# Interleaving half layers of eight experts with attention work, and moving the gate decision of a batch into the next batch's block

## What is computed

```
h = conv(x, cos(phases) * w_real - sin(phases) * w_imag)      # (8, 735, 64)
n = layernorm(h)
h = h + softmax((n Wq^T)(n Wk^T)^T / 8) n                     # attention, values are n itself
n = layernorm(h)
logits = n gate_w + gate_b                                    # (8, 735, 16)
weights, index = softmax(top_k(logits, 2))
moe = sum over the two: weight * (relu(n w1[e] + b1[e]) w2[e] + b2[e])
h = h + layernorm(n + moe) * gamma + beta
```

## Time and profile before

| what | us |
|---|---|
| median of 3 runs | 396.76 |
| lowest and highest run | 396.74, 397.37 |
| the profiled execution, whole | 397.81 |
| its span, first to last instruction | 396.0 |
| PE busy | 373.5 (94%) |
| DVE busy | 247.5 (62%) |
| ACT busy | 159.0 (40%) |
| POOL busy | 141.8 (36%) |

### The profile page before, as it was taken

The page is one execution under the profiler, slowest core; times in us unless marked ns, Lnnn a source line. Parts: engine busy times, 40 slices in busy tenths (PEclk is TensorE's granted clock), DMA queues, the critical chain, the costliest instruction groups (busy, mean ns, idle before and its releaser), DMA issues.

```text
span 396.0 us, 6294 instructions
## 1 busy us (share of the span) xinstructions
PE 373.5 (94%) x2222; PEld 244.7 (62%) x2222; DVE 247.5 (62%) x592; ACT 159.0 (40%) x494; POOL 141.8 (36%) x167
## 2 busy tenths in 40 slices
PE   8879999889999999999999999999989999999992
PEld 6336475575658666676667755576657667657660
DVE  3377568874686646763776536765676446967662
ACT  3364253363337533354346543374344453020022
POOL 5110040310661185324761165513860296015062
PEclk9998999999999999999999999999999999999997
DMA  5800000392003940079000980059102969539301
GB/s 156 196 33 0 2 1 2 136 406 112 1 2 85 407 183 2 1 246 397 33 1 11 334 330 0 2 160 407 69 1 65 392 231 357 208 102 407 126 2 40
DMA packets 23135, 55.92 MB, mean 141 GB/s; under 512 B 3776, under 2 KB 5312, under 8 KB 22976
## 3 DMA queue, kind: packets, MB, share of 16 engines
q1 hardware_dynamic: 23104, 55.53, 38.6%
HBM read 53.57 MB, written 1.95 MB: 140 GB/s over the span
## 4 chain that ended last, share of the span: by engine, by line
PE 78%; DVE 9%; ACT 5%; SPq 3%; issue 2%; DMA 2%; POOL 1%; POOLq 0%; ACTq 0%; DVEq 0%
PE mix L1070 22%; PE wide L1070 18%; PE up L1070 17%; PE small L1070 15%; DVE row_max L846 3%; PE wide L1096 2%; ACT probs L629 2%; DMA bet<-beta 2%; PE wide L1193 1%; PE small L1089 1%; PE wide L1145 1%; ACT relu L621 1%; DVE probs L913 1%; ACT cen_sq L584 1%; POOL hidden L363 1%
## 5 line engine op out<-in xcount | busy, mean ns | idle before, releaser
L913 DVE SCALAR_TENSOR_TENSOR hidden<-up,b_neg,gates_all 128x368 f32<-128x368 f32 x128 | 70.8, 594 | 22.2 <-PE up L1070 22.1
L1070 PE MATMUL up<-x,w_hi 128*128 128x368 f32 x198 | 74.5, 376 | 1.7 <-ACT relu L621 1.5
L1070 PE MATMUL mix<-hidden,w2s 128*64 128x368 f32 x400 | 67.4, 475 | 0.7 <-POOL hidden L363 0.6
L488 POOL TENSOR_TENSOR rstd<-var_eps,power 128x6 f32<-128x6 f32 x24 | 31.9, 1329 | 94.1 <-ACT cen_sq L584 94.1
L1070 PE MATMUL up<-x,w_lo 128*128 128x368 f32 x198 | 65.3, 330 | 0.0
L363 POOL TENSOR_TENSOR hidden<-relu,gates_all 128x368 f32<-128x368 f32 x52 | 48.9, 976 | 21.4 <-ACT relu L621 21.4
L1070 PEld LDWEIGHTS up<-x,w_hi 128*128 128x128 f32 x198 | 37.1, 188 | 18.9 <-ACT relu L621 6.2
L1070 PEld LDWEIGHTS mix<-hidden,w2s 128*64 128x64 f32 x400 | 27.5, 136 | 33.0 <-issue 28.3
L629 ACT ACTIVATE probs<-wide 128x736 f32<-128x736 f32 (+2 forms) x48 | 36.5, 780 | 25.3 <-PE wide L1070 25.3
L846 DVE TENSOR_REDUCE row_max<-wide 128x1 f32<-128x736 f32 (+1 forms) x48 | 42.7, 916 | 5.9 <-PE wide L1070 5.6
L584 ACT ACTIVATE cen_sq<-cen 128x65 f32<-128x65 f32 x144 | 34.8, 246 | 8.5 <-DVE cen L860 3.4
(11 more groups left out here) (186 smaller groups left out, 547.5 us busy)
## 6 DMA issues: line engine op xcount, KB each, us to landing
gates_all<-gates_far SPq DMA_DIRECT2D x128, 368.0 KB, 7.7
xt<-x_t SPq DMA_DIRECT2D x8, 375.0 KB, 8.4
out<-outs SPq DMA_DIRECT2D x8, 192.0 KB, 1.9
w_raw<-w SPq DMA_DIRECT2D x2, 512.0 KB, 6.2
w2s<-w SPq DMA_DIRECT2D x1, 512.0 KB, 7.2
gates_far<-gates_t SPq DMA_DIRECT2D x8, 46.0 KB, 1.7
gates_all<-w_real SPq DMA_DIRECT2D x2, 128.0 KB, 2.8
gates_all<-w_imag SPq DMA_DIRECT2D x2, 128.0 KB, 3.3
```

Of the source, the lines that this page charges most:

```text
L488: pool.tensor_tensor(rstd[k][:], var_eps[k][:], power[:], ALU.pow).then_inc(s_rstd[k], 1)
L913: dve.scalar_tensor_tensor(hidden_of(n, e)[:, s, :], up_of(n, e)[s], b1_neg[:, e:e + 1], gates_all[:, e, s * HALF:(s + 1) * HALF], ALU.max ...
L1070: return pe.matmul(dst, lhsT, rhs, start=start, stop=stop, skip_group_check=True)
```

## The change

Five things change, and no instruction of the arithmetic is added or taken away.

1. **Halves.** `first_layer`, `scores`, `max_scores`, `project`, `to_features` and `gate_logits` can be called by half. In `common_block` and in the second part of `iteration`, PE alternates a half of a first layer with a half of something else. Before, it issued a whole first layer and then a whole score tile.
2. **The gate decision moves.** The logits of batch i-1 stand in the first block of iteration i, into `small`; `top_two(i - 1)` stands there ahead of `hide(m, 0)`, and `top_places` and `gate` behind `hide(m, 3)`. Before, all of it stood in the last stage of iteration i-1.
3. **Tile 3 of the scores** goes behind the first half of expert 0, and tile 3 of the maxima goes into the last stage. The maxima of the tiles 2 to 5 all use `wide0` now, and `MAX_FREE` makes each wait for the one before it.
4. **Expert 9** leaves `POOLED`: DVE does its hidden layer, and in the last stage `hide(m, 9)` stands ahead of `x2_lo`.
5. **`gate_room`** is always `gate_space`, which lies in SBUF. Before, it lay in PSUM (`wide1`) for most batches.

The diff, cut to its core:

```diff
-POOLED = (4, 5, 8, 9, 10)
+POOLED = (4, 5, 8, 10)
...
-MAX_BUF = (0, 1, 0, 1, 0, 0)
-MAX_FREE = (0, 0, 1, 2, 3, 5)
+MAX_BUF = (0, 1, 0, 0, 0, 0)
+MAX_FREE = (0, 0, 1, 3, 4, 5)
...
-            room = small[:, 2 * NT * E:BANK] if n == BATCH - 1 else gate_space[:] if n == 1 else wide[1][:, 1, :]
+            room = gate_space[:]
...
-                    exponentials(i, 0, 4)
+                    exponentials(i, 0, 3)
...
                     mix_copy(before)
+                    exponentials(i, 3, 4)
                     mix_tokens(before)
-                    exponentials(i, 4, NT)
+                    exponentials(i, 4, 5)
+                    exp_gap(i - 1)
+                    exponentials(i, 5, NT)
...
+                rectify(m, POOLED[2])
                 if conv:
                     x2_hi(i, i % 3)
-                for e in POOLED[2:]:
-                    rectify(m, e)
+                rectify(m, POOLED[3])
...
+                if not first:
+                    top_two(i - 1)
...
+                top_places(i - 1)
+                gate(i - 1)
...
                 next_max(i, 0)
+                hide(m, 6)
                 next_max(i, 1)
-                hide(m, 6)
+                hide(m, 7)
                 next_max(i, 2)
-                hide(m, 7)
-                next_max(i, 3)
                 second_normed(i)
 
-                x2_lo(i, i % 3)
-                next_max(i, 4)
                 for e in range(8, 11):
                     hide(m, e)
-                top_two(i)
+                x2_lo(i, i % 3)
+                next_max(i, 3)
+                next_max(i, 4)
+                hide(m, 11)
                 next_max(i, 5)
-                hide(m, 11)
-                top_places(i)
-                gate(i)
...
-                pe.wait_ge(s_gates, i)
                 transpose_gates(m)
-                first_layer(before, 12)
-                scores(i, 0)
...
+                first_half(before, 12, 0)
+                score_half(i, 0, 0)
+                first_half(before, 12, 1)
+                score_half(i, 0, 1)
...
+                first_half(before, 15, 0)
...
+                gate_logits(i - 1, small, FORE)
+                first_half(before, 15, 1)
+                gate_logits(i - 1, small, REAR)
...
+                first_half(m, 0, 0)
+                score_half(i, 3, 0)
+                first_half(m, 0, 1)
+                score_half(i, 3, 1)
...
+                first_half(m, 4, 0)
                 attention_to_tokens(i)
-                first_layer(m, 4)
...
+                first_half(m, 4, 1)
+                next_max(i, 0, 0)
+                first_half(m, 5, 0)
+                next_max(i, 0, 1)
```

More of the change, by code:

```diff
@@ L42 @@
 E, F = 16, 128
-POOLED = (4, 5, 8, 9, 10)
+POOLED = (4, 5, 8, 10)
 HIDDEN = 4
 QUAD = 4
+FORE, REAR = range(NT // 2), range(NT // 2, NT)
 PART = 4
@@ L884, in gate @@
                 g = 8 * i
-                at, wsum, wtop, second = gate_room(i)
+                at, wsum, wtop, second = gate_room()
                 dve.wait_ge(s_topi, NT * i + NT)
@@ L944, in iteration @@
                     keys_lo(i + 1)
-                if first:
-                    top_places(1)
-                    gate(1)
+                if not first:
+                    top_two(i - 1)
                 for e in range(4 if first else 0, 4):
                     hide(m, e)
-                if conv:
+                if conv and not first:
+                    query_lo(i + 1)
+                top_places(i - 1)
+                gate(i - 1)
+                if first:
                     query_lo(i + 1)
@@ L1090, in to_tokens, with to_features @@
                 last.then_inc(done, 1)
-            def to_features(dst, src, done):
-                for t in range(NT):
+            def to_features(dst, src, done, tiles=range(NT)):
+                for t in tiles:
                     w, j = tile_size(t), t // 2
@@ L1114, in keep_awake, with max_half @@
                     mm(mix[:, 0:P], ident[:], ident[:], True, True)
-            def max_scores(i, t, buf, reduced):
-                if t == 0:
+            def max_half(i, t, buf, reduced, s):
+                if s == 0 and t == 0:
                     pe.wait_ge(s_qhi, i + 1)
@@ L1122, in max_scores @@
                     pe.wait_ge(s_klo, i + 1)
-                elif t == 1:
+                elif s == 0 and t == 1:
                     pe.wait_ge(s_qlo, i + 1)
-                else:
+                elif s == 0:
                     pe.wait_ge(s_max, NT * i + reduced)
                 a, w = tile_start(t), tile_size(t)
-                lhs = q_hi[:, a:a + w]
-                mm(wide[buf][0:w, 0, 0:HALF], lhs, keys[i % 2][:, 0:HALF], True, True)
-                mm(wide[buf][0:w, 1, 0:HALF], lhs, keys[i % 2][:, TOK - HALF:TOK], True, True).then_inc(s_rough, 1)
+                k = s * (TOK - HALF)
+                last = mm(wide[buf][0:w, s, 0:HALF], q_hi[:, a:a + w], keys[i % 2][:, k:k + HALF], True, True)
+                if s == 1:
+                    last.then_inc(s_rough, 1)
+            def max_scores(i, t, buf, reduced):
+                for s in range(2):
+                    max_half(i, t, buf, reduced, s)
             def bias_product():
@@ L1146, in transpose_max, with score_half, scores @@
                 last.then_inc(s_maxt, 1)
-            def scores(i, t):
-                if t == 0:
+            def score_half(i, t, s):
+                if s == 0 and t == 0:
                     pe.wait_ge(s_shift, i + 1)
-                elif t >= 2:
+                elif s == 0 and t >= 2:
                     pe.wait_ge(s_prob, NT * i + (TURNS_FREE if i < AHEAD else SCORE_FREE)[t])
                 a, w = tile_start(t), key_size(t)
+                cols = slice(s * HALF, (s + 1) * HALF)
+                dst = wide[score_buf(i, t)][0:w, s, 0:HALF]
+                mm(dst, keys[i % 2][:, a:a + w], q_hi[:, cols], True, False)
+                last = mm(dst, keys1[i % 2][:, a:a + w], q_lo[:, cols], False, True)
+                if s == 1:
+                    last.then_inc(s_score, 1)
+            def scores(i, t):
                 for s in range(2):
[L1156 to L1159, removed]
+                    score_half(i, t, s)
             def weigh_values(i, t, buf):
@@ L1178, in attention_to_tokens, with gate_logits @@
                 last.then_inc(s_at, 1)
[L1180 to L1183, removed]
+            def gate_logits(i, dst, tiles=range(NT)):
+                if tiles[0] == 0:
+                    pe.wait_ge(s_x2lo, i + 1)
+                    pe.wait_ge(s_w1lo, 1)
+                for t in tiles:
                     a = tile_start(t)
@@ L1186, in gate_logits @@
                               gw[:].rearrange("p a e -> p (a e)"), True, True)
-                last.then_inc(s_lg, 1)
+                if tiles[-1] == NT - 1:
+                    last.then_inc(s_lg, 1)
             def transpose_gates(i):
```

143 lines of the change are left out of this document (84 added, 59 removed).

## The result

The changed kernel takes **407.15 us** (median of 4 runs, 405.07 to 408.94), the kernel before on the same chip 396.75 (4 runs, 396.47 to 397.37). The ratio is 1.0247 [1.0219, 1.0275] (the ratios here are those on record, with their 95% intervals; quotients of the medians differ from them by up to 0.0023). The sign was as forecast, and so was the wait that makes about half of the time. The size was not: +10.4 us where the sum had +6.0, and above the upper end of the range. One later run of the kernel before, at 426.91 us and a mean clock of 0.846, was in a slower state and is in no ratio.

A forecast was written before the change was run, and what follows sets the result against it. PE, busy 94%, was taken to bound the kernel, with some 3.6 us of handoffs an iteration. Last-stage stalls less smaller gains summed to +6.0 us on 396.8, so 402.8 us; own range 400 to 405.5, 8-in-10 range 399.5 to 406.5.

The forecast's parts named there:

- the sum: Whole run: +1.3 in iteration 2, +1.6 each in 3 to 5, +0.4 in 6, -0.5 in 7; +6.0 us.
- The stall at tile 4: Last stage, iterations 2 to 6: PE waits 1.9 us for the maximum of tile 3; +1.8 us each.
- The walk through DVE's list: Last stage: expert 9's hidden pair to 3.35 us, `x2_lo` to 4.25, maximum of tile 3 to 5.15.
- Experts 4 to 7: Stage after the first `second_layers`: 5.44 us for 5.65, -0.2; in iteration 2, -0.5.
- The first block: Start of an iteration: 0.6 us of handoffs saved pays for the logits moved in; net 0.
- `gap` and `gate_space`: Gate decision on DVE: `gap` takes 0.20 us without holding PE; `gate` reading SBUF beside POOL's `gamma_beta` costs 0.
- the first rival: Gate decision holds up the attention: six instructions alternate with POOL's, 1 us more in iterations 3 to 6; 407, chance 0.13.
- One of the prediction's own signs of being wrong: In the changed profile, the instructions of `gate` on DVE would take 0.9 us each.
- Iteration 6: Last stage +1.8 us, less 1.4 for vanished waits for POOL's hidden layers and the gates; +0.4 us.
- Iterations 2 and 7: Iteration 2: +1.3 us, from -0.5 in experts 4 to 7 and +1.8 in the last stage; iteration 7: -0.5 us.
- The third rival: No difference: last stage costs only +0.7 us, first block gives -0.6, within 0.8 us of 396.8; chance 0.04.

The follow-up runs named there:

- the run with the filler: Changed kernel with five matmuls of a zero weight, adding nothing to mix, put into PE's wait for the maximum of tile 3; 402.67 us, ratio 1.0127.

## Where the prediction was right, and where it was wrong

- **The stall at tile 4** was right, to the tenth: 1.82 us for 1.9, 7.68 for 7.7 in the stage, in five iterations out of five. The walk through DVE's list was made link by link from rows, and the two experiments that took a link out shortened the wait, by 1.1 us (`x2_lo`) and 1.0 (expert 9).
- **Experts 4 to 7** take 5.36 us in iteration 3 (142.43 to 147.79), for 5.44 forecast. Right.
- **The first block** costs nothing, as forecast. In iteration 4 it goes from 167.24 to 182.47, 15.23 us for 15.27 before, with the logits in it:

```profile
167.24 0.42 PE L1073 MATMUL up<-x,w_hi 128*128 128x368 f32 x1
...
182.47 3.94 PE L1073 MATMUL small<-probs,xn 128*64 128x368 f32 x24
...
292.26 2.08 PE L1073 MATMUL mix<-hidden,w2s 128*64 128x368 f32 x12 [0.70 <-POOL hidden L364]
```

- **`gap` and `gate_space`.** DVE in iteration 4 of the changed kernel, and below it POOL's `gamma_beta` at that time:

```profile
177.07 0.17 DVE L879 TENSOR_TENSOR gap<-top 128x6 f32<-128x6 f32 x1
...
186.40 0.91 DVE L902 TENSOR_TENSOR gate_space<-pick,gate_space 128x96 f32<-128x96 f32 x1
...
187.35 1.04 DVE L905 TENSOR_TENSOR gates<-pick,gate_space 128x96 f32<-128x96 f32 x1
...
190.74 0.20 DVE L857 RECIPROCAL rden<-small 128x6 f32<-128x6 f32 x1 [2.35 <-PE small L1073]
```

```profile
186.37 0.83 POOL L494 TENSOR_TENSOR res<-cen,rstd 128x384 f32<-128x384 f32 x1
187.28 1.00 POOL L496 TENSOR_TENSOR res<-res,gam 128x384 f32<-128x384 f32 x1
```

  `gap` took 0.17, for 0.20 forecast and 0.92 in its old place. Two of the six instructions of `gate` do take turns with POOL: 0.91 and 1.04 us, each ending where one of POOL's ends (187.31 beside 187.20, 188.39 beside 188.28). The rule of the Trainium skill (SBUF — State Buffer, "Who interferes with whom"), that a DVE instruction with two SBUF inputs and a GpSimd instruction that reads SBUF exclude each other, agrees with these two rows. But the first rival needed the attention to wait for it, and DVE stood idle for 2.35 us behind them, ahead of `rden`. So nothing of it reached PE: that the rival's 407 is the measured time is luck. One of the prediction's own signs of being wrong, instructions of `gate` at 0.9 us, came true for two of the six, and it cost nothing.
- **Iteration 6** was right: +0.4 forecast, 0.5 measured without its stretch at low clock. The waits of 0.57 and 0.44 are gone, and one of 0.70 for POOL's hidden layers has come in ahead of `second_layers(m, 4)` (292.26 above), which the prediction didn't see. The sum also left out the -0.2 of the experts 4 to 7 here, so the agreement is partly luck.
- **Iterations 2 and 7** were off by 0.4 and 0.3 us in opposite senses. The third rival (no difference) doesn't add up on its own terms: +0.7 for the last stage and -0.6 for the first block, with the rest of the forecast, make some -1 to -2 us.
- **The step that failed** is the sum itself: it turned each 1.9 us of standing into 1.8 us of time and priced all work behind it at 0.17 us a matmul. It had no term for the clock, though the earlier trace rows showed that this kernel can lose it: the fourth slice of the page reads 8. Behind the wait of 1.82 us matmuls started 0.30 us apart for 3.4 us, at a granted clock of 0.50. The missing term is 1.0 to 1.3 us for each time that the clock fell, three times in the profiled run and by estimate four or five in the median, 4.8 us by the run with the filler. With the waits as measured (5.4 for the 6.0 forecast) and the filler's 4.8 the sum is 396.8 + 5.4 + 4.8 = 407.0, beside the 407.15 measured. A smaller step failed behind it: none of the rivals had a price in clock for a wait, so the range ended at 406.5.

**Open** is why the waits of 1.82 us in iterations 2 and 3 weren't followed by the low clock in the profiled run, while those of 1.32 were in all five iterations of one other kernel and those of 1.48 in four of another. Open as well is why one wait of 0.95 brought it in one profiled run and not in nine others. The runs show which lengths can bring it, not what decides in a single case.

## What to carry to other kernels

When an edit puts a wait on an engine that is nearly always busy, price the wait and then what may follow it: here 1.3 to 1.8 us of standing were followed by the low clock in 12 of 15 cases, at 1.0 to 1.5 us for a single stretch, while behind 0.65 to 0.85 the profiles show none. Look at the list of the engine that is waited for before giving up the edit: the loss sat in two entries of DVE's list (a hidden pair and `x2_lo`) ahead of one maximum, and a change of their order and owner turned +2.5% into -0.8%. And read the clock of the kernel before: a single lower digit in it says that this term exists. Compare runs at like mean clock where a difference is of the size of one low stretch.

## What the runs showed of the hardware

The granted clock of PE fell from 2.4 to 1.2 GHz for some 3.4 us at short stops in otherwise dense work, from some 0.7 us before the end of the wait to some 2 us after it. By the length of the longest wait:

| kernel | wait of PE in the last stage, us | iterations of 5 with the clock at 0.5 there (profiled run) |
|---|---|---|
| changed, expert 9 on POOL and tile 3 first | 0.46 | 0 |
| the same with whole pieces | 0.53 | 0 |
| before with one spare reduction | 0.65 | 0 (but lower mean clocks in two other runs) |
| changed, tile 3 first | 0.74 | 0 |
| changed, expert 9 on POOL | 0.85 | 0 |
| changed, whole pieces | 1.32 | 5, one of double length |
| before with two spare reductions | 1.48 | 4, one of double length |
| changed | 1.82 | 3 |
| changed, wait filled with zero products | 0.19 | 0 |

That multiplying by a weight of zeros is enough to hold the clock, and pays for itself, was not expected. The second surprise is how local the low clock is. Windows of 8 us of the changed kernel, both from 0.5 us ahead of the end of the wait, in iteration 3 and in iteration 4:

```profile
157.00:165.00 8.00, 7.36 (x44) 3.91 (x46) 3.30 (x5) 1.04 (x2) 2.30 (x3) 1.00 0.00 0
204.00:212.00 8.00, 7.52 (x36) 4.33 (x38) 3.30 (x5) 1.05 (x2) 2.29 (x3) 0.79 0.00 0
```

PE's busy time is no lower (7.5 for 7.4 us) where the clock is lower, while it starts 36 matmuls in place of 44. So a column of busy shares hides the loss that the clock's column shows.
